# State-space matrices built from 0/1 columns on all partitions, one backward-stepping copy, zeros by a transfer, and 1.5 token tiles in each gate piece

## The reference, cut to what matters

```python
xn = _layernorm(x)
u = einsum(xn, W_x) + b_x;  g = sigmoid(einsum(xn, W_g) + b_g)
u = u * g + conv3(u) * (1 - g)
dt = clip(softplus(einsum(xn, W_dt) + b_dt).mean((0, 1)), 0.001, 2.0)
A = -softplus(A_raw);  A_d = exp(A * dt[:, None]);  B_d = (A_d - 1) / (A + 1e-6) * B_ssm
# scan over the 256 steps of a sequence
state = A_d * state + B_d * u_t;  y_t = sum_s(state * C_ssm)
attn = _layernorm(xn + y @ W_out.T + b_out) * ln_g + ln_b
h = int(xn[:, 0] + xn[:, 1]) mod 8;  experts h and (h + 1) mod 8, each weighted by 1/2
ffn = sum over the two of relu(xn @ W1[e] + b1[e]) @ W2[e] + b2[e]
out = x + attn + ffn
```

## Time and profile before

| | us |
|---|---|
| median of 3 runs | 472.11 |
| lowest and highest | 470.94, 472.18 |
| the profiled execution, its own time | 472.0 |
| its span in the trace | 470.2 |
| PE, PEld, DVE busy | 417.2, 368.6, 394.6 |
| ACT, POOL busy | 316.2, 240.2 |
| granted clock of PE, mean | 0.986 of full |

### The profile page before, as it was taken

One profiled execution on the slowest core, in us unless ns is written; L12 is line 12 of the kernel. 1 busy time (PEld: TensorE's weight loads), 2 busy tenths in 40 slices (PEclk: granted clock), 3 DMA queues, 4 the chain that ended last, 5 costly groups with the idle time before them and its releaser, 6 DMA issues. The chain is left out here.

```text
span 470.2 us, 11677 instructions
## 1 busy us (share of the span) xinstructions
PE 417.2 (89%) x3387; PEld 368.6 (78%) x3387; DVE 394.6 (84%) x666; ACT 316.2 (67%) x898; POOL 240.2 (51%) x272
## 2 busy tenths in 40 slices
PE   1047899999998989999999999979999999999991
PEld 1035788887998989999999999979999555568880
DVE  6989776775649999999999999989992549997997
ACT  2686799998875667787655567566555666546873
POOL 4595777777424132343263253652422577777740
PEclk9999999999899989999999999999999999999997
DMA  9998334622322112112232233432222638189544
GB/s 236 255 413 280 98 117 125 174 77 82 90 45 45 33 33 44 41 39 45 40 84 49 43 88 92 108 84 47 43 42 45 182 92 233 56 213 246 169 129 135
DMA packets 111418, 52.78 MB, mean 112 GB/s; under 512 B 48881, under 2 KB 106393, under 8 KB 111385
## 3 DMA queue, kind: packets, MB, share of 16 engines
q1 hardware_dynamic: 106328, 43.48, 35.3%
q0 software_dynamic: 4096, 8.40, 5.8%
q10 hardware_dynamic: 960, 0.52, 0.4%
HBM read 28.12 MB, written 24.25 MB: 111 GB/s over the span
## 5 line engine op out<-in xcount | busy, mean ns | idle before, releaser
L1449 PE MATMUL PS<-AR 128*128 128x128 f32 x1184 | 140.2, 277 | 4.9 <-ACT AR L768 4.9
L1449 PEld LDWEIGHTS PS<-AR 128*128 128x128 f32 x1184 | 137.0, 194 | 5.5 <-ACT AR L768 5.5
L768 ACT ACTIVATE AR<-PS,VC 128x256 f32<-128x256 f32 x296 | 112.4, 490 | 4.7 <-PE PS L1437 4.0
L1435 PE MATMUL PS<-XT,RR 128*128 128x256 f32 x296 | 86.6, 292 | 3.6 <-POOL XT L581 3.5
L1436 PE MATMUL PS<-XT,RR 128*128 128x256 f32 x296 | 83.3, 282 | 0.0
L1437 PE MATMUL PS<-XT,RR 128*128 128x256 f32 x296 | 83.2, 281 | 0.0
L581 POOL TENSOR_TENSOR XT<-XTX,XT 128x256 fp32r<-128x256 f32 x35 | 33.4, 956 | 91.2 <-ACT XT L745 91.2
L575 POOL DMA_INDIRECT sorted_tokens<-RA,posi x64 | 62.2, 972 | 23.6 <-issue 11.3
L605 POOL TENSOR_TENSOR AR<-AR,b2p 128x256 f32 x37 | 36.5, 988 | 56.7 <-ACT AR L781 53.7
L781 ACT ACTIVATE AR<-PS 128x128 f32 x74 | 16.5, 274 | 68.8 <-PE PS L1449 63.7
L1435 PEld LDWEIGHTS PS<-XT,RR 128*128 128x128 f32 x296 | 56.3, 190 | 4.9 <-POOL XT L581 4.5
(11 more groups left out here) (231 smaller groups left out, 851.4 us busy)
## 6 DMA issues: line engine op xcount, KB each, us to landing
sorted_tokens<-AR SPq DMA_DIRECT2D x10, 512.0 KB, 5.6
XTX<-sorted_tokens SPq DMA_DIRECT2D x160, 32.0 KB
sorted_outputs<-AR SPq DMA_DIRECT2D x37, 128.0 KB, 1.9
RA<-in_L_attn_x_dram SPq DMA_DIRECT2D x8, 512.0 KB, 8.2
normalised_tokens<-RA SPq DMA_DIRECT2D x16, 256.0 KB
RB<-normalised_tokens SPq DMA_DIRECT2D x8, 512.0 KB, 7.0
AR<-in_L_ffn_W_dram SPq DMA_DIRECT2D x15, 256.0 KB, 3.4
out_dram<-RB SPq DMA_DIRECT2D x7, 512.0 KB, 3.3
```

Source lines behind the costliest of these rows:

```text
L768: nc.scalar.activation(HID[n][:, k, :], ps[2 * n + k // 2][:, (k % 2) * FT:(k % 2 + 1) * FT], ACT.Relu, bias=B1C[:, e, k:k + 1]).then_inc( ...
L1435: T.matmul(bank, W1h[slot][:, w], XT[:, 0:FT], start=True, stop=False)
L1449: ins = T.matmul(ps[5 + h][:, 0:D], HID[n][:, k, h * P:(h + 1) * P], W2S[slot][:, k, :], start=(n == 0 and k == 0), stop=(n == 1 and k == ...
```

## The change

- The pace in the gate pieces becomes `(10 * j + 64) // 20`, 1.5 tiles a piece.
- The 24 memsets on DVE go. READ's half of RB is cleared by one transfer of 128 x 16 KB from a row of zeros in DRAM, which ACT issues in iteration TZERO = 27; the row is written once near the start by SP from the ZERO tile (one transfer of 16 KB), and SP waits for it before it loads over ZERO. DVE waits for the cleared half ahead of the first L1213. INTRA and INJ need no clearing, as each of their elements is now written.
- ACT computes the powers in iteration 26 instead of 25.
- The 32 copies of L1163 become one copy of 128 x 2048, whose source steps backward by one for each row.
- The eight copies of 32 partitions into INTRA become four multiplications of 128 partitions by a column of `odd` (1 in odd quarters, else 0, and the reverse); the eight into INJ become eight multiplications of 128 partitions by a column of `quad` (1 in one quarter). Two small instructions build these columns.
- The calls of `tiles_to` among the matrices are placed anew.

```diff
-                return (10 * j + 67) // 21
+                return (10 * j + 64) // 20
...
+            sp.dma_start(zero_dram.rearrange("o (r c) -> (o r) c", c=2 * CH), ZERO[0:NTOK // (4 * CH), :]).then_inc(s_zrow, 16)
...
+                    with act.If(i == TZERO):
+                        act.wait_ge(s_gdone, 1)
+                        act.wait_ge(s_zrow, 16)
+                        act.dma_start(RB[:, 1, NTOK // 2:NTOK], zero_dram.broadcast_to([P, NTOK // 2])).then_inc(s_rzero, 16)
...
-            tiles_to(27)
-            for n in range(3 * NTOK // 2 // CH):
-                hb, c = (0, n * CH) if n < NCH // 2 else (1, n * CH - NTOK // 2)
-                V.memset(RB[:, hb, c:c + CH], 0.0)
-                if n in (11, 23):
-                    tiles_to(28 + n // 12)
+            tiles_to(28)
...
-            for j in range(Q):
-                ins = V.tensor_copy(TO[:, :, :, j], KP[:, :, Q - 1 - j:2 * Q - 1 - j])
-            link(ins)
+            lag0 = KP[:, :, Q - 1:Q]
+            link(V.tensor_copy(TO, bass.AP(lag0.tensor, lag0.offset, [lag0.ap[0], lag0.ap[1], (1, Q), (-1, Q)])))
...
-            for q in range(NQ):
-                r = slice(Q * q, Q * q + Q)
                 for hb in range(HB):
-                    ins = V.tensor_copy(IN5[r, hb, :, q % 2, :], TT[r, hb])
-                if q % 2:
-                    tiles_to(32 + q // 2)
-            link(ins)
+                    V.tensor_scalar(IN5[:, hb, :, w, :], TT[:, hb], odd[:, w:w + 1], None, ALU.mult)
...
-                    ins = V.tensor_copy(INJ5[r, hb, :, q, :], IT[r, hb])
+                    ins = V.tensor_scalar(INJ5[:, hb, :, q, :], IT[:, hb], quad[:, q:q + 1], None, ALU.mult)
+                if q == 1:
+                    tiles_to(33)
...
+            tiles_to(35)
+            dve.wait_ge(s_rzero, 16)
```

30 lines of the change are left out of this document (20 added, 10 removed).

## The result

| | before | after |
|---|---|---|
| median | 472.12 us | 477.18 us (476.22 to 477.51, 4 runs) |
| ratio, 95% interval | | 1.0109, 1.0088 to 1.0131 |
| profiled execution, its span | 472.0, 470.2 us | 477.37, 475.6 us |
| last output copy of the tile stage (iteration 36) | 364.22 us | 369.55 us |
| from there to the end of the span | 106.0 us | 106.1 us |

A forecast was written before the change was run, and what follows sets the result against it. PE was taken to bound most of the tile stage, with DVE mattering only where a tile comes late. From 472.0 us, -3.3 - 0.2 (tile 17) - 0.4 + 1.5 = -2.4 gave 469.6 us, range 467.8 to 473.2.

The forecast's parts named there:

- Tile 7 and the clock: Gate pace, iterations 4 to 7: tile 7 comes earlier and PE's clock stays up; -3.3 us (between -1.7 and -3.7).
- Tile 35: Iterations 34 and 35, behind the gates: the only tile late there comes in time; -0.4 us.
- DVE's savings on the matrices: Memsets and copies on DVE: about 19 us saved, none on the path, since PE's work covers it.
- Stage 3: Stage after the tile stage: keeps its old length, with the tile stage over near 361.8 us.
- the zero transfer: Iteration 28's wait for weights: 2.93 MB at 410 GB/s, weights landing at 308.9 instead of 307.4; +1.5 us (0 to +7.4).
- the other end: Upper bound of the zero-transfer term: at 226 GB/s 13.0 us, to 314.0, plus 0.8 to landing; +7.4 us.
- Rival (a): Zeros in iteration 27 take the weights' time at 226 GB/s and the clock falls; 477.1 us, chance 0.12.
- near 296: Expected issue time of the zero transfer in the changed kernel's profile, all being 4 us earlier by then.
- 256 KB would hardly wait: Weights beside the zeros: by packet turns between queues alone, the term would be nearer 0 than 1.5 us.
- The 6.7 against 1.9 us: Start of kernel: ACT's 128 KB beside SP's loads took 6.7 us to landing, alone 1.9; taken to show sharing hurts.
- how long the low part of tile 7 would take: POOL before iteration 7: low part at most 1.66 us beside two-input DVE instructions, 0.73 at best; done by 164.4.
- Iterations of 6.37 us to the end of the gate pieces: Expected in the changed kernel's profile: iterations keep 6.37 us until the gate pieces end.

The follow-up runs named there:

- experiment 4: Kernel before with one edit: the zero transfer in iteration 27 in place of eight of its 24 memsets; 477.3 us, ratio 1.0124.
- experiment 8: Changed kernel with the bias-row chain shortened and group 0's preparation spread over iterations 8 to 10, zeros in iteration 27; 477.94 us, ratio 1.0141.
- experiment 2: Changed kernel with the zero transfer at iteration 30 instead of 27; 471.41 us, ratio 0.999 against the kernel before.
- experiments 6, 7 and 9: Changed kernel, zeros at 30: bias rows only for group 0, 465.71 us; shorter bias chain, 470.13 (spread: 470.37); spread with low weights behind bias add, 465.99.

## Why the prediction was wrong

**Right.** Tile 7 and the clock: 0.29 us of wait for its transpose (at 161.32) instead of 3.04, clock 1.00 from 160 to 180, iteration 7 ended at 170.3 us (forecast 171.3). The term was -3.3 us; in the runs that started at 124.5, iterations 4 to 7 took 27.3 us instead of 31.0, -3.7. Tile 35 gave its 0.4 us. DVE's savings on the matrices were worth nothing: DVE idles 17 us between 280 and 350 (52.77 busy of 70), and waits for loaded tiles, as said. Stage 3 kept its length.

**The term that was mis-sized: the zero transfer.** It stood in the sum with +1.5 us and bounds of 0 to +7.4; iteration 28 grew by 5.5, and the transfer alone costs 5.8 (experiment 4) or 7.6 (experiment 8). The step that failed is the last of its working: it took all 2.93 MB as one stream at 410 GB/s, through at 308.1. The zeros were indeed through near 308. But of SP's bytes only 0.24 MB had passed by then, and the rest, the weights among it, came behind: 0.97 MB at 264 and 227 GB/s, the slow rate that I had named as the other end. The issue itself was held up too: L422 took 1.58 us at 302.00, and 0.50 in experiment 2, so L418 was issued 1.1 us later than there. The delay of the weights was 4.1 us instead of 1.5, and 1.4 us more came from the clock at its lower level: PE's L1456 took 5.23 us, where L1449 had taken 3.84. Rival (a) had the long wait and the low clock, with a chance of 0.12, but its reason, the zeros themselves at 226 GB/s, is wrong. The prediction had one rate for everything, the fast or the slow one; the zeros at the fast rate and then the weights at the slow one was not among its cases. It should have had a good chance, and the low clock with it: in each run of the chips that take 471 us the clock fell to 0.50 in iteration 28 when zeros were issued in 27, with half of them too. The issue came at 301.08, not near 296, because the 4 us won ahead had been lost again by then; the landing of 2 MB has 8.5 us, and by that, as an estimate, any issue between 296 and 303 meets the weights.

The Trainium skill ("DMA: Bandwidth & Descriptors", section "Queues, rings and completion order") has each transfer engine take turns between queues by packets, and I made of it that 256 KB would hardly wait. The same section gives a packet typically 9 to 17 descriptors. The trace counts 144 records for the zeros; over the 16 engines that would be 9 for each, so by that rule each engine's share of the zeros could be one packet, and what comes behind would wait for all of it. The trace agrees in that SP's queue moved next to nothing while the zeros passed, but it doesn't show the packets themselves. The 6.7 against 1.9 us that I took as a sign of sharing compared a load with a store, so it said less than I made of it.

**What was left out: POOL's chain.** The prediction followed the pace through DVE, ACT and PE, and of POOL it asked only how long the low part of tile 7 would take. It did name the lengthening (1.66 us instead of 0.73 beside two-input instructions), and did not ask which other POOL instruction PE's earlier arrival would bring beside the gate pieces. At the start of groups 1 and 2 it is a chain of five, on whose end SP's store, load and weights hang. It costs 1.25 + 0.7 + 3.4 us at iterations 19, 25 and 26, of which 1.8 are the clock in 26 (10.65 against 8.86 without its fall). This is shown by the pace alone (the longer iterations appear), the old pace (they go), and the bias rows left out and the instructions moved (they go, with the gain of the pace kept). "Iterations of 6.37 us to the end of the gate pieces" was the line in the prediction that this refutes.

The time was near rival (a)'s 477.1, but not for its reason alone: (a) counted a gain of 3.9 us and a loss of 9, and the kernel has a gain of 5.5 (5.5 and 1.3 in the iterations, less 1.3 for the later start), a loss of 5.3 at the group starts and one of 5.5 at the zeros. That the two differences come out alike, 5.1 and 5.3 us, is luck.

Left open: why the clock falls at 292 in the changed kernel, and in the run with the zeros at 30 only in iteration 28, though PE was idle for as long at 290 (0.16 and 0.21 us busy of 2). In iteration 28 all runs in which the chain was shortened gained 2 us or more against experiment 2. Of that 1.6 us are the clock, which stays at 1.00 there in the runs of experiments 6, 7 and 9 that started at 124.4 to 125.7; the rest is a wait for the weights of 1.65 to 2.53 us instead of 3.00, and why they come earlier was not followed row by row.

## What to carry to other kernels

When an engine is made to run ahead, go through every engine that follows it and ask what its instructions will then lie beside; a gain at one boundary of a loop is lost at the next where a short chain on POOL gates the queue that loads the next weights. A large transfer with long rows, issued here 0.9 to 2.7 us ahead of a small one on another queue that somebody waits for, held it back until nearly all of it was through: put such a transfer where no load is awaited, and don't count on the other queue to part them. And what is ahead of a store or a load in an engine's order should be the shortest it can be, with the long instruction that nobody waits for behind it.
